# Sums of squared q and k through folding DMAs, and DRAM fills moved from the first attention to the second

## The reference

```python
q = _silu(x @ Wq)
k = _silu(x @ Wk)
v = _silu(x @ Wv)
q = _causal_dwconv(q, conv_q_w)
k = _causal_dwconv(k, conv_k_w)
v = _causal_dwconv(v, conv_v_w)
q = q * cos + rot_half(q) * sin
k = k * cos + rot_half(k) * sin
q = q / jnp.maximum(jnp.linalg.norm(q, axis=-1, keepdims=True), 1e-12)
k = k / jnp.maximum(jnp.linalg.norm(k, axis=-1, keepdims=True), 1e-12)
for s in range(K):
    attn = jnp.einsum('bshd,bshd->bsh', q, _lag(k, s)) * scale
    out = out + (attn * jax.nn.sigmoid(_lag(a, s) * b))[..., None] * _lag(v, s)
```

## Time and profile before

| what | value |
|---|---|
| median of 3 runs | 1094.26 us |
| the profiled execution | 1096.4 us, of which its span is 1094.6 us |
| PE, DVE, ACT, POOL busy | 92%, 68%, 51%, 26% of the span |
| first attention, turns 2 to 14 | PE busy without a gap, 21.3 us a turn |
| L686, the sums of squares | 512 PE instructions, 63.9 us, 5% of the chain that ended last |
| rope DMAs, L1924 | 64, 256 KB each, 5.6 us to landing (median) |
| fills, L513 and L515 | 16 of 576 KB and 16 of 256 KB, 4.4 us to landing |

### The profile page before, as it was taken

The page is one execution under the profiler, slowest core; times in us unless marked ns, Lnnn a source line. Parts: engine busy times, 40 slices in busy tenths (PEclk is TensorE's granted clock), DMA queues, the critical chain, the costliest instruction groups (busy, mean ns, idle before and its releaser), DMA issues.

```text
span 1094.6 us, 16914 instructions
## 1 busy us (share of the span) xinstructions
PE 1011.9 (92%) x5768; PEld 804.6 (74%) x5768; DVE 749.7 (68%) x1303; ACT 554.1 (51%) x1097; POOL 284.2 (26%) x246
## 2 busy tenths in 40 slices
PE   6989999999999999999979999999988996589987
PEld 4778998998899854354468988989885454278876
DVE  4778999899899869972477787877873154423444
ACT  2558877877887788711155565555641123023220
POOL 1034334423433401030112112121100005536660
PEclk9989999999999999989989999999998998789997
DMA  7097867877867940430011011111002002278845
GB/s 224 3 218 152 192 147 158 172 170 154 167 159 167 255 112 0 158 83 0 7 52 58 29 58 46 41 58 29 29 0 73 0 1 87 81 229 271 275 134 196
DMA packets 78461, 121.59 MB, mean 111 GB/s; under 512 B 25091, under 2 KB 54606, under 8 KB 77776
## 3 DMA queue, kind: packets, MB, share of 16 engines
q1 hardware_dynamic: 66384, 86.91, 26.3%
q0 software_dynamic: 12032, 34.11, 15.7%
HBM read 70.31 MB, written 38.08 MB: 99 GB/s over the span
## 4 chain that ended last, share of the span: by engine, by line
PE 79%; DVE 10%; DMA 3%; ACT 3%; issue 3%; POOL 2%; POOLq 0%; SPq 0%; ACTq 0%; DVEq 0%
PE psum L632 9%; PE psum L633 9%; PE psum L634 9%; PE psum L857 5%; PE psum L1040 5%; PE psum L686 5%; PE psum L999 5%; PE psum L804 4%; PE psum L882 3%; PE psum L764 3%; PE psum L745 3%; PE psum L1050 2%; PE psum L813 2%; PE psum L675 2%; DVE arena L1492 2%
## 5 line engine op out<-in xcount | busy, mean ns | idle before, releaser
L1492 DVE SCALAR_TENSOR_TENSOR arena<-arena,par_in 128x1024 f32<-128x1024 f32 x144 | 183.5, 1283 | 33.3 <-ACT arena L1122 23.6
L632 PE MATMUL psum<-G_r,arena_r 128*128 128x512 f32 x320 | 132.7, 415 | 7.2 <-DVE G_r L1585 4.1
L633 PE MATMUL psum<-G_r,arena_r 128*128 128x512 f32 x320 | 127.9, 400 | 0.0
L634 PE MATMUL psum<-G_r,arena_r 128*128 128x512 f32 x320 | 127.5, 399 | 0.0
L1924 POOL DMA_DIRECT2D arena<-arena x64 | 53.8, 983 | 210.4 <-DVE arena L1504 210.2
L1270 ACT ACTIVATE arena<-psum,small 128x256 f32<-128x256 f32 x128 | 59.3, 473 | 87.3 <-DVE small L1650 87.3
L1112 ACT ACTIVATE arena<-psum 128x1024 f32<-128x1024 f32 x48 | 49.2, 1026 | 62.6 <-PE psum L634 62.0
L632 PE MATMUL psum<-arena_r 128*128 128x256 f32 x256 | 78.0, 305 | 2.2 <-DVE arena_r L1675 1.5
L632 PEld LDWEIGHTS psum<-G_r,arena_r 128*128 128x128 f32 x320 | 61.3, 191 | 21.4 <-DVE G_r L1585 4.9
L1940 POOL TENSOR_TENSOR arena_r<-arena,arena_r 128x512 fp32r<-128x512 f32 x16 | 20.7, 1293 | 214.5 <-ACT arena_r L1239 214.5
L1973 POOL DMA_INDIRECT out_rows<-arena x64 | 62.2, 973 | 47.7 <-DVE arena L1825 25.3
(11 more groups left out here) (238 smaller groups left out, 2375.1 us busy)
## 6 DMA issues: line engine op xcount, KB each, us to landing
arena<-arena POOLq DMA_DIRECT2D x64, 256.0 KB, 5.6
arena<-in_w_moe SPq DMA_DIRECT2D x33, 384.0 KB, 3.7
slot_rows<-nowhere SPq DMA_DIRECT2D x16, 576.0 KB, 4.4
arena<-slot_rows SPq DMA_DIRECT2D x32, 288.0 KB, 3.8
arena<-bands SPq DMA_DIRECT2D x16, 528.0 KB, 4.3
sq_rows<-arena POOLq DMA_DIRECT2D x16, 512.0 KB, 7.4
arena<-in_w_qkvz SPq DMA_DIRECT2D x16, 384.0 KB, 3.7
arena<-in_qkv_codes SPq DMA_DIRECT2D x16, 384.0 KB, 3.2
```

What stands on the lines that cost most here:

```text
L632: nc.tensor.matmul(dst, w_l, x_h, start=start, stop=False, skip_group_check=True)
L633: nc.tensor.matmul(dst, w_h, x_l, start=False, stop=False, skip_group_check=True)
L634: return nc.tensor.matmul(dst, w_h, x_h, start=False, stop=stop, skip_group_check=True)
L1492: nc.vector.scalar_tensor_tensor(by_batch(dst), by_batch(u[s])[:, :, j:j + S], par_in[:, bass.ds(M_CW + (w * H + h) * TAPS + j, 1)], by_ba ...
```

## The change

The squares of k are made right after those of q, ahead of silu of z. GpSimd then issues a DMA that adds the upper 64 rows of the squares of q to the lower 64 (each row of 1024), and one that adds the lower rows of the squares of k to the upper; it waits for both to land and issues a third that copies k's 64 rows under q's, all of it ahead of the rope DMAs of the turn. TensorE then makes the sums of both in 8 products instead of 16, at the start of the next turn, against a block whose first column has ones in the rows of q and whose other columns have ones in those of k. VectorE sets that block with four memsets in turn 0. The two fills leave SP's turns of the first attention and follow each head's load in the second.

```diff
@@ SP: the two fills leave turn() and go behind load1
+            def fill(h):
+                sp.dma_start(slot_rows...[h], nowhere...).then_inc(sg("moe_fill"), 16)
+                sp.dma_start(out_rows...[h], nil...).then_inc(sg("moe_fill"), 16)
+            fill(0)
             with sp.Fori(1, H) as h:
                 sp.wait_ge(sg("a1_wmul"), h)
                 load1(h)
+                fill(h)
@@ PE, at the start of stage 2 (was: wait a0_sq_k, 8 products of k)
+                    pe.wait_ge(sg("a0_sq_qk"), 16 * h)
+                    if since(h, 2):
+                        pe.wait_ge(sg("a0_ssq_s"), h - 1)
                     for i in range(NT):
+                        m = nc.tensor.matmul(bank(7)[:, 2 * i:2 * i + P], sqq[:, i * P:i * P + P], by_pair,
                                              start=True, stop=True, skip_group_check=True)
+                    m.then_inc(sg("a0_ssq"), 1)
@@ PE, ahead of project_q
-                if 1 in st:
-                    pe.wait_ge(sg("a0_sq_q"), h + 1)
-                    if since(h, 1):
-                        pe.wait_ge(sg("a0_ssq_s"), h)
-                    squared_sums(0, "q")
@@ ACT
                 if 1 in st:
                     squared("q")
+                    squared("k")
                     ...silu of z, 8 scalings of v...
-                if 1 in st:
-                    squared("k")
@@ DVE
+                    nc.vector.tensor_scalar(ssq_s.rearrange("p (s i) -> p s i", s=2),
+                                            bank(7)[:, 0:2 * NT].rearrange("p (i s) -> p s i", s=2), 1e-24, None, ALU.max)\
+                        .then_inc(sg("a0_ssq_s"), 1)
+                    for q_rows in range(2):
+                        r = slice(0, P // 2) if q_rows else slice(P // 2, P)
+                        nc.vector.memset(by_pair[r, 0:1], float(q_rows))
+                        i = nc.vector.memset(by_pair[r, 1:P], float(1 - q_rows))
@@ POOL, ahead of the rope DMAs
+                    pool.wait_ge(sg("a0_sq_q"), h + 1)
+                    nc.gpsimd.dma_start(sqq[low, :], sqq[high, :], accum_op=ALU.add).then_inc(sg("a0_fold"), 16)
+                    pool.wait_ge(sg("a0_sq_k"), h + 1)
+                    nc.gpsimd.dma_start(sqk[high, :], sqk[low, :], accum_op=ALU.add).then_inc(sg("a0_fold"), 16)
+                    pool.wait_ge(sg("a0_fold"), 32 * (h + 1))
+                    nc.gpsimd.dma_start(sqq[high, :], sqk[high, :]).then_inc(sg("a0_sq_qk"), 16)
```

More of the change, by code:

```diff
@@ L126, in build @@
         ident, ones, inv_d = cst[:, C_ID:C_ID + P], cst[:, C_ONE:C_ONE + P], cst[:, C_INV:C_INV + P]
-        strict = cst[:, C_STRICT:C_STRICT + P]
+        strict, by_pair = cst[:, C_STRICT:C_STRICT + P], cst[:, C_MASK:C_MASK + P]
         half_scale, seam = 0.5 * SCALE, cst[:, C_SEAM:C_SEAM + PAD]
@@ L512, in turn @@
                         load_z(hh + 1)
[L513 to L516, removed]
             sp.wait_ge(sg("pool_fill"), 1)
@@ L556, in _ @@
                     .then_inc(sg("in_wo"), 16)
+            def fill(h):
+                sp.dma_start(slot_rows.rearrange("(h p r) c -> h p r c", h=H, p=P)[h],
+                             nowhere.unsqueeze(1).broadcast_to([P, SLOTS // (H * P), ROW])).then_inc(sg("moe_fill"), 16)
+                sp.dma_start(out_rows.rearrange("(h p r) c -> h p r c", h=H, p=P)[h],
+                             nil.unsqueeze(1).broadcast_to([P, T * TOPK // (H * P), D])).then_inc(sg("moe_fill"), 16)
+            fill(0)
             with sp.Fori(1, H) as h:
@@ L681, in project0 @@
                     return halves0(dst, par, j, n)
-                def squared_sums(j, s):
+                if 2 in st:
+                    if is_last(h, 1):
+                        pe.wait_ge(sg("a_sb"), 7)
+                    pe.wait_ge(sg("a0_sq_qk"), 16 * h)
+                    if since(h, 2):
+                        pe.wait_ge(sg("a0_ssq_s"), h - 1)
                     for i in range(NT):
-                        n = j * NT + i
-                        m = nc.tensor.matmul(bank(7)[:, n:n + P], sqr[s][:, i * P:i * P + P], ones,
+                        m = nc.tensor.matmul(bank(7)[:, 2 * i:2 * i + P], sqq[:, i * P:i * P + P], by_pair,
                                              start=True, stop=True, skip_group_check=True)
[L688 to L692, removed]
+                    m.then_inc(sg("a0_ssq"), 1)
                 if 1 in st:
@@ L1518, in turn @@
                         dve.wait_ge(sg("a0_rqk"), h - 1)
-                    nc.vector.tensor_scalar(ssq_s, bank(7)[:, 0:2 * NT], 1e-24, None, ALU.max).then_inc(sg("a0_ssq_s"), 1)
+                    nc.vector.tensor_scalar(ssq_s.rearrange("p (s i) -> p s i", s=2),
+                                            bank(7)[:, 0:2 * NT].rearrange("p (i s) -> p s i", s=2), 1e-24, None, ALU.max)\
+                        .then_inc(sg("a0_ssq_s"), 1)
                 if is_last(h):
@@ L1538, in turn @@
                     gates_scaled()
+                    for q_rows in range(2):
+                        r = slice(0, P // 2) if q_rows else slice(P // 2, P)
+                        nc.vector.memset(by_pair[r, 0:1], float(q_rows))
+                        i = nc.vector.memset(by_pair[r, 1:P], float(1 - q_rows))
+                    i.then_inc(sg("a_sb"), 1)
                 if 2 in st:
@@ L1919, in turn @@
                 if 1 in st:
+                    low, high = slice(0, P // 2), slice(P // 2, P)
+                    pool.wait_ge(sg("a0_sq_q"), h + 1)
[4 more added lines that the diff above has]
+                    nc.gpsimd.dma_start(sqq[high, :], sqk[high, :]).then_inc(sg("a0_sq_qk"), 16)
                     for s in "qk":
```

## The result

The changed kernel takes **1131.4 us** (median of 4 runs, 1130.46 to 1131.71) against 1094.01 us before it (median of 4, 1091.65 to 1094.26): a ratio of **1.0335, 95% interval 1.0316 to 1.0355**. It is slower, as forecast, but by 37 us and not by 14, and it lies 9 us above the top of the range.

What follows compares the result with a forecast made beforehand. PE was busy throughout turns 2 to 14; the new turn was to follow ACT's loop or the DMA chain. Turns +7.6 and end +6.5 made +14.1 us on the 1094.26 median: 1108.4 us, range 1096 to 1122.

Steps and rivals of the forecast that it cites:

- The loop through ACT: Silu of v through scalings and q projection to the next silu: 21.67 us a turn against 21.30, 0.37 longer.
- PE's idle time before the q projection: PE stands idle about 2.2 us ahead of each q projection, until ACT's scalings of v end; a sign to check.
- rival C: The fills delay turn 1's weights, so moving them makes the kernel faster: 1089 us; chance 0.07.
- rival B: Folds meet other transfers every turn, 1.3 us more each, end 8 to 11: 1120 to 1123 us; chance 0.18.
- The folds and the copy in a turn: The next turn's sums wait for these DMAs and can start again at 21.4 us, 22.0 in odd turns.
- The end: At the first attention's end, head 15's folds and copy meet SP's 4.2 MB of loads: +6.5 us, bounds 0 and 11.
- the prediction's two cases: Head 15's folds share the engines with SP's loads, +3.3 us, or queue up behind all of them, +8.0 us.
- the copy's 3.5 us: Landing time of the copy of k's squares, taken from the first rope DMA; bounds 2.5 and 4.4 us.
- round-robin between the two kinds of queue: The skill's rule for DMA engines, giving 3.3 us at the first attention's end; the prediction leaned to order of arrival.
- The fills and turn 1: Moving the fills costs nothing, and turn 1's wait for weights covers the first copy: 0, bounds -8 and +2.
- A: Only ACT's loop counts, folds and copy are quick, the end is shared: 1099.5 to 1102.8 us; chance 0.24.
- D: Turns stay within 0.1 us of 21.30 and the end's folds slip in: 1094 to 1096 us; chance 0.07.

Runs made afterwards that it cites:

- e2: The kernel before with only ACT's squares of k moved right behind those of q; ratio 1.0082 to the kernel before.
- f2: The changed kernel without its three folding DMAs a head, with 8 constant products where the sums of q had been; ratio 1.0058 to the kernel before.
- e5: The changed kernel without its three new DMAs a head, everything else the same; ratio 1.0178 to the kernel before.
- f1: The changed kernel again, unaltered, on another chip; ratio 1.0325 to the kernel before.
- e3: The kernel before with the 8 products for the sums of q left out after turn 0; ratio 0.9944 to the kernel before.
- e4: The changed kernel with 8 constant products, never read, where the sums of q had been; ratio 1.0192 to the kernel before.
- f4: The kernel before with all 16 products for the sums moving 4 columns of ones instead of 128; ratio 1.0005 to the kernel before.
- e6: The changed kernel with all five of SP's loads at the first attention's end held until the last copy landed; ratio 1.0282 to the kernel before.
- e1: The kernel before with only the two DRAM fills moved to the second attention, behind each head's load; ratio 0.9986 to the kernel before.
- e9: The changed kernel with ACT's old order, sums behind the k projection, and SP's last three loads held until the copy landed; ratio 1.0483 to before.

## Why the prediction was right in sign and wrong in size

**The loop through ACT: right.** 0.37 us a turn was worked out, and e2 and f2 measured 0.37 (21.67). It accounts for 13 x 0.37 = 4.8 us of the 17.5.

**PE's idle time before the q projection: seen, and never priced.** The prediction says that PE stands idle about 2.2 us there in each turn, and looks for that as a sign. It was there, 23.1 us in twelve waits, 1.9 us each. What was missing is the next step: what TensorE's clock does behind such a wait. This is the step of the prediction that failed first: it put that cost at nothing in the turns, without a reason. I had a row for it in hand, the clock of 0.56 behind an idle 4.93 us in turn 1, and used it only for 3 us in the end's upper bound and in rival C. The changed kernel's six turns with a stretch at the lower clock take 139.8 us, 9.8 more than six of 21.67; in e5, with eight, it is 12.4 us against f2. So the 17.5 us of the turns are 4.8 of ACT's loop, 9.8 of the clock and 3.0 of the folds, to 0.1 us. The other rival for the same time, that the folds bind hard (rival B, which 1120 to 1123 belonged to), falls with e5: taking out all folds shortened the mean turn by 0.01 us against the profile after and by 0.25 against f1, not by 1.3. So the time came out on B's side, 8 us above it, but not by B's mechanism.
The Trainium skill (TensorE: Matmul & The Clock Gate, section "HAM oscillation — how this bites in real kernels") describes a kernel that throttles and recovers again and again because of a wait in each step of its loop. The runs here agree with that picture in part: behind 1.9 us of waiting once a turn the clock fell in 6 to 8 turns of 13, not in each, and behind 1.0 us (e3) in none.

**The folds and the copy in a turn: about right in size, and partly hidden.** I took 3.5 us for the fold of q, 4.75 for that of k (17.65 less 12.90) and 3.5 for the copy. The rows of their three lines over turns 2 to 14, twelve DMAs each, in this order (minimum, median, maximum):

```profile
DMA to landing us min/median/max: 3.5/3.9/4.9
...
DMA to landing us min/median/max: 4.1/5.2/6.4
...
DMA to landing us min/median/max: 2.9/3.7/5.8
```

Each median is 0.2 to 0.5 us longer than I took. With a full clock the turns are then 0.46 us above ACT's loop (e4 against f2) where 0.17 was predicted. That turns 2 to 14 of the changed kernel sum to 294.45 us and e5's to 294.36 is luck: e5 had eight turns with a stretch at the lower clock, the changed kernel six. In f1 it had eight too, and its sum is 297.57, 3.2 above e5's. The Trainium skill's sum for a DMA issued by GpSimd (DMA: Bandwidth & Descriptors, section "Anatomy of one DMA"), from which the prediction estimated 2.6 us, is below the shortest of all of them, 2.9; the measurement decides, and had it held, e4 should have had the turns of f2.

**The end: right mechanism, half the size.** 6.5 us was taken within 0 to 11; it is 13.3 in the profiled execution and 10.4 in f1 (53.1 less 42.66). The end varies without any fold as well: 42.8 in e5, 43.1 in f2, but 46.1 in f4, where the clock over it is 0.89. The prediction let the two folds wait behind SP's 4.2 MB. Issued at 387.22 and 388.16, the second landed at 398.3, 10.1 us after its issue: between the prediction's two cases, 7.3 us if the folds share the engines and 13 if they queue up behind all the loads. The step that failed is the copy's 3.5 us, taken from the quiet turns (4.4, a fill's, in the other case). It took 8.7, because it met the loads again. With nothing of SP's ahead, in e6, it took 2.9; here it was issued at 398.56, and from 399 to 402 only packets of SP's went. The queues' packets from 399 to 402 (packets, MB, share), where there is no row for POOL's queue at all:

```profile
q1 hardware_dynamic: 191, 1.25, 100.6%
```

SP needs 4.95 us, from 388.54 on, to issue the last load, and that load landed 19.0 us after its issue: SP's queue still had work when the copy came. To which load the packets ahead of the copy belong, the trace doesn't tell. The rope DMAs of that place, 7.3 to 9.5 us, had it in them: I used them for the folds and not for the copy as well. The rest is the clock again: TensorE ran at the lower level for 13.7 us from 398.7 on, from within the 11.27 us of waiting to 412.4, and the sums took 3.78 us instead of 2.05. From the sums to S it is 419.47 - 407.25 = 12.2 us, where I had counted 10.0 without the idle time.
The Trainium skill's round-robin between the two kinds of queue (DMA: Bandwidth & Descriptors, section "SWDGE vs HWDGE vs iDMA"), by which the end would have been 3.3 us, isn't what this row shows. From 391 to 397, while the folds went, packets of both queues went (158 of POOL's, 643 of SP's), and the folds were late all the same; e6 shows that the loads ahead are what delays them.

**The fills and turn 1: right.** 0 was predicted for the fills (e1: none), and the wait in turn 1 stays (9.20 us now, 8.26 before; on other chips 6.93 in e1 without the fills and 5.81 in f4 with them), so rival C falls. Turn 2 starts 0.6 us later.

**Rivals A and D.** A needed the folds hidden and a shared end. The folds were hidden in part, and yet the turns were long. D needed turns of 21.30, and e2 rules it out.

By its own terms the prediction had 7.0 us for these 13 turns and 6.5 for the end; they measure 17.5 and 13.3. What stays open is why the clock fell in some turns and not in others behind the same wait, and seldom behind the longer waits of e9.

## What to carry to other kernels

Work on the engine that is busy all the time is worth its duration only if nothing waits beneath it: look for what ends just before the group would, since here 1.0 of the 1.8 us covered a wait (e3), and the order made for the new scheme turned it into 1.9. When an edit leaves TensorE idle once in every turn of a loop, price the clock behind that wait as well as the wait, and test it with products that nobody needs: if these make the kernel faster, it was the clock. A chain of DMAs that stands in place of a little engine work has to be costed at its worst place in the program, each link of it, with what the other queues have just issued.

## What I had not expected of the hardware

- An idle stretch of TensorE of 1.9 to 2.1 us once in a turn of 21.7 us was followed by 3.4 us at a granted clock of about 0.55 in 6 to 8 turns of 13, and each such turn was 1.6 us longer (e5: 23.2 against 21.67). With 1.0 us (e3) and with the gap filled (f2) it stayed at 1.00 in these turns. With 2.9 to 3.2 us in every second turn and 1.4 us in each (e9) it fell in two turns only.
- Eight products added to each turn made the kernel faster: 1.0192 against 1.0335, and 1.0058 against 1.0178 without the folds.
- Eight fp32 products with 4 moving columns took as long as eight with 128 (f4): their 16 weight loads filled the same 1.86 us.
- DMAs of 256 KB from SBUF to SBUF that landed in 3.5 to 4.7 us by themselves (e6) took 8.5 to 10.1 behind SP's loads of 4.2 MB.
